# Attention pass 2 taken two key chunks at a time, with P·V four chunks behind the scores

## The chip, the cores and the metric

The kernel runs as one program on all 8 cores of one Trainium2 chip. The metric is the device time of one execution, in microseconds (us), of the slowest core. Every core does the same amount of work, on its own 2,048 tokens.

## The reference

A transformer layer on x of shape (4, 4096, 1024): attention with 16 heads of 64, then a feed-forward network. Cut to what matters here:

```python
qk = einsum(q * d**-0.5, k)              # scores, per head
exp_qk = exp(qk - max(qk))
out = (exp_qk @ v) / sum(exp_qk)
x = x + layernorm((out + q) @ Wo + bo)
x = x + layernorm(ffn(layernorm(x)))     # silu, gelu, gelu; 1024 -> 4096 -> 4096 -> 4096 -> 1024
```

Each core takes the queries of half a sequence (2,048) against all its 4,096 keys.

## The kernel before

The attention part loops over 8 pairs of heads (`hp`). For each pair, `emit_kv` projects K and V of all 4,096 keys, and the queries follow in 4 tiles of 512 (`qt`). A query tile has two passes.

**Pass 1** (`pass1_steps`) finds the maximum of each query's scores. It is a list of 69 steps. The first makes the query slices ready: a VectorE copy for one head, a DMA for the other. 64 steps are alike: one score matmul (L593) into the PSUM tile psP1a or psP1b, by turns; one VectorE cast out of it (L598); one VectorE minimum of the negated scores (L602, a TENSOR_SCALAR with an accumulated result, which the trace shows as TENSOR_SCALAR_CACHE_REDUCE and DVE_READ_ACCUMULATOR). After each 16 of these stands one step (`th2`) with two small reductions (L615), each followed by a DMA of GpSimd (L619) that writes the column of maxima into the row that pass 2 reads as the 65th row of its queries. The second reduction waits for the first one's DMA, since both work on the buffer `b_gc`. So the four `th2` are steps 17, 34, 51 and 68, counted from 0.

**Pass 2** (`emit_pass2`) computes the attention itself, over 32 chunks of 128 keys. For a chunk `kc` it issues:

- ST: two score matmuls (L651), one for each head, into psST0 (even chunks) or psST1 (odd chunks), each a PSUM tile of 128x1024
- two steps from the pass 1 of the *next* query tile (`nxt`), where there is one
- PV: two matmuls (L637) of chunk `kc-2`, which add P·V of the two heads into psPVa and psPVb
- exp: one ScalarE activation (L662) from psST into a bf16 buffer P, of which there are three (`b_pt`), taken by `kc % 3`

After the 32 chunks stand the two last PV, the leftover 5 steps of pass 1, and the division: two reciprocals (L668, L670), two broadcast matmuls (L672, L675), copies, products and sums on VectorE. Written in the order of the program, the division comes before the leftover steps.

The tiles `qt` 0 to 2 of each pair carry pass 1 of the next tile within their pass 2. I call these 24 tiles *stepped*. The tile `qt` 3 has none, and I call these 8 *plain*. The pass 1 of tile 0 runs by itself, after `emit_kv`.

The order on each engine is the order in which `p.op` is called. Waits are derived from the buffers that an op reads and writes: an op that reads a buffer waits for its last writer *so far in that order*, and an op that writes one waits for the last writer and for all that have read it since. Each engine counts its ops in one semaphore, and a wait is left out where the engine has already waited for the same or a later count. TensorE runs its matmuls in order.

Of the kernel before, what the change touches and what calls it, by code (L numbers as in the profile page):

```python
# [10 lines left out]
AF = mybir.ActivationFunctionType  # L11
# [212 lines left out]
def build_program(cfg):  # L224
# [4 lines left out]
    NKC = Tf // 128  # L229
# [28 lines left out]
    with stack:  # L258
        E = stack.enter_context
        p = Prog(nc, stack)  # L260
# [8 lines left out]
        PB = Pool(nc, stack, "PB", BF16, pb_elems)  # L269
# [9 lines left out]
        psST0 = E(nc.psum_tensor("psST0", [128, 1024], F32))  # L279
        psST1 = E(nc.psum_tensor("psST1", [128, 1024], F32))  # L280
# [5 lines left out]
        bST = [p.buf(f"psST{i}", True) for i in range(4)]  # L286
# [8 lines left out]
        def slot():  # L295
# [23 lines left out]
            reads=[bccol], writes=[bbks])  # L319
# [35 lines left out]
        b_pt = [p.buf("pt0"), p.buf("pt1"), p.buf("pt2")]  # L355

        def PTof(par):
            return o_pt0 if par == 0 else o_pt_m + (par - 1) * 1024
        scpy = [PB.view(o_scpy + i * 512, 512) for i in range(2)]
        b_scpy = [p.buf("scpy0"), p.buf("scpy1")]  # L360
        b_qg = [p.buf("qg0"), p.buf("qg1")]
        b_qgg = [p.buf("qgg0"), p.buf("qgg1")]
        b_kb1, b_kb2 = p.buf("kb1"), p.buf("kb2")
        qgv = [PB.view(o_qg + i * 512, 512) for i in range(4)]
# [67 lines left out]
        for tc in range(NTC_F if not cfg.get("skip_a1") else 0):  # L432
# [7 lines left out]
            for i in range(ND):  # L440
# [5 lines left out]
                    reads=[ab, b_stats], writes=[b_xln[i]], tag="ln1ap")  # L446
# [110 lines left out]
        def k65(h, kc):  # L557
            if h == 0:
                return PB.t[0:65, o_k + kc * 128:o_k + (kc + 1) * 128], [b_k]
            if kc * 128 < 2048:  # L560
                return PB.t[0:65, o_kb1 + kc * 128:o_kb1 + (kc + 1) * 128], [b_kb1]
            return PB.t[0:65, o_kb2 + kc * 128 - 2048:o_kb2 + (kc + 1) * 128 - 2048], [b_kb2]
# [65 lines left out]
        def emit_pass2(hp, qt, nxt):  # L628
# [4 lines left out]
            def emit_pv(kc):  # L633
                par = kc % 3
                for h in range(2):
                    psv, bpv = (psPVa, bPVa) if h == 0 else (psPVb, bPVb)
                    p.op("tensor", lambda t, kc=kc, h=h, par=par, psv=psv: t.matmul(  # L637
                        psv[:, :], V_hp[kc][:, h * 65:h * 65 + 65],
                        PB.t[:, PTof(par) + h * 512:
                             PTof(par) + (h + 1) * 512],  # L640
                        start=(kc == 0), stop=(kc == NKC - 1)),
                        reads=[b_v[kc], b_pt[par]], writes=[bpv],
                        war_free=(kc > 0), tag="pvMM")

            for kc in range(NKC):
                par = kc % 2
                pst = psST0 if par == 0 else psST1
                bsth = [bST[2 * par], bST[2 * par + 1]]
                for h in range(2):
                    lhsT, lbuf = k65(h, kc)  # L650
                    p.op("tensor", lambda t, h=h, pst=pst, lhsT=lhsT: t.matmul(  # L651
                        pst[:, h * 512:(h + 1) * 512], lhsT,
                        qgv[gsl * 2 + h][0:65, :],
                        start=True, stop=True),
                        reads=lbuf + [b_qg[gsl], b_qgg[gsl]], writes=[bsth[h]], tag="stMM")
                for _ in range(2):
                    if nxt:
                        nxt.pop(0)()
                if kc > 1:
                    emit_pv(kc - 2)  # L660
                par3 = kc % 3
                p.op("scalar", lambda s, par3=par3, pst=pst: s.activation(  # L662
                    PB.t[:, PTof(par3):PTof(par3) + 1024],
                    pst[:, :], AF.Exp), reads=bsth, writes=[b_pt[par3]], tag="exp")
            emit_pv(NKC - 2)
            emit_pv(NKC - 1)
            rd = PF.view(o_rd, 1024, 64, 65)
            p.op("vector", lambda v: v.reciprocal(rd[:, 0:512], psPVa[64:65, :]),  # L668
                 reads=[bPVa], writes=[b_rd, b_big1], tag="recipA")
# [339 lines left out]
```

How the kernel before makes its waits and increments, by code:

```python
            def body(eng):  # L164
                watermark = {}
                for o in prog.ops[e]:
                    for d in o.deps:
                        if d[0] == "eng":
                            sem = prog.sems[d[1]]
                            val = prog.ops[d[1]][d[2]].sem_val
                            assert val is not None, (d, o.tag)
                        else:
                            sem = d[1].handle
                            val = d[2]
                        key = id(sem)
                        if watermark.get(key, -1) >= val:
                            continue
                        watermark[key] = val
                        eng.wait_ge(sem, val)
                    inst = o.fn(eng)
                    if o.dma_sem is not None:
                        inst.then_inc(o.dma_sem.handle, 16)
                    elif o.inc:
                        inst.then_inc(prog.sems[e], 1)
```

## Time and profile before

| | us |
|---|---|
| median of the 2 runs shown (8253.65 to 8258.03) | 8255.84 |
| the profiled execution's own time | 8252.05 |
| its span on the slowest core, core 7 | 8250.5 |
| spans of the 8 cores | 8229.1 to 8250.5 |
| mean granted TensorE clock, share of full speed | 0.706 to 0.708 |
| busy: TensorE matmul, VectorE, ScalarE, GpSimd | 5968.2, 3807.9, 1593.4, 778.5 |

The span begins with layer norm and the Q projection (to about 440 us), goes on with the 8 pairs of heads (to about 5250 us, some 601 us for each), and ends with the output projection and the feed-forward network. "Idle before, with a releaser" in a row says how long the engine had nothing to do ahead of that instruction, and which instruction's end released it. The granted clock is a share of 2.4 GHz: 1.0 is 2.4 GHz and 0.5 is 1.2 GHz. All rows are of core 7.

### The profile page before, as it was taken

The numbers are of one execution on the slowest core, as the hardware profiler recorded it, in microseconds if no ns is written. First come the engines' busy times: TensorE is split into PE (matmuls) and PEld (weight loads), VectorE is DVE, ScalarE is ACT, GpSimd is POOL, SyncE is SP. The second block draws the span as 40 slices with busy tenths as digits, with TensorE's granted clock in tenths as the row PEclk, the third lists the DMA queues.
The fourth block names the chain that finished last, engine by engine and source line by source line (L and its number), as shares of the span: only waits on it lengthen the run. The fifth ranks groups of instructions, "written<-read, shape, count | busy, mean of one in ns | idle before, by whom it ended". The sixth has DMA issues, their size and how long they took to land.

```text
span 8250.5 us, 84474 instructions; the slowest of 8 cores (8229.1 to 8250.5 us)
## 1 busy us (share of the span) xinstructions
PE 5968.2 (72%) x21520; PEld 2117.6 (26%) x21520; DVE 3807.9 (46%) x8231; ACT 1593.4 (19%) x1826; POOL 778.5 (9%) x991
## 2 busy tenths in 40 slices
PE   2447657756756756756657657549899987999995
PEld 0111121211211211211211211214344433444442
DVE  7567667567577477577477577551100012000002
ACT  0212312312312312312212212213000002200000
POOL 0000000000000000000000000001222221122222
PEclk6765565655655655655655655769999998999998
DMA  3000000000000000000000000136677797677787
GB/s 42 13 1 1 3 1 1 3 1 1 3 1 1 3 1 1 4 1 1 4 1 1 4 1 11 46 87 72 79 76 77 77 90 110 72 76 76 77 80 97
DMA packets 820344, 267.87 MB, mean 32 GB/s; under 512 B 721304, under 2 KB 797344, under 8 KB 819872
## 3 DMA queue, kind: packets, MB, share of 16 engines
q0 software_dynamic: 796208, 218.27, 26.9%
q1 hardware_dynamic: 23664, 44.20, 1.7%
q8 instruction: 187, 3.06, 0.2%
q14 instruction: 285, 2.33, 0.1%
HBM read 461.60 MB, written 16.78 MB: 58 GB/s over the span
## 4 chain that ended last, share of the span: by engine, by line
PE 64%; DVE 18%; DMA 9%; issue 7%; ACT 1%; DVEq 0%; POOLq 0%; POOL 0%; ACTq 0%; SPq 0%
PE psST L868 21%; PE psST L651 8%; DVE PB L598 7%; PE psP1a L593 6%; PE psP1b L593 5%; DMA PB<-PF 5%; PE psPVa L637 5%; PE psPVb L637 4%; PE psST L819 3%; PE psST L812 3%; PE psST L896 2%; PE psST L524 2%; DVE PB L602 2%; DMA PB<-w3t 2%; DVE PF L670 1%
## 5 line engine op out<-in xcount | busy, mean ns | idle before, releaser
L868 PE MATMUL psST<-PB 128*128 128x512 bf16 x8192 | 1773.7, 380 | 16.3 <-DMA PB<-h1t 16.3
L662 ACT ACTIVATE PB<-psST 128x1024 bf16<-128x1024 f32 x1024 | 1032.7, 1023 | 3292.4 <-PE psST L651 3291.4
L602 DVE TENSOR_SCALAR_CACHE_REDUCE PB<-PB 128x512 bf16<-128x512 bf16 x2048 | 1405.2, 686 | 264.2 <-DVE PB L598 7.2
L651 PE MATMUL psST<-PB 65*128 65x512 bf16 x2048 | 980.4, 578 | 338.8 <-DMA PB<-PF 333.9
L593 PE MATMUL psP1a<-PB 64*128 64x512 bf16 x1024 | 602.6, 588 | 743.6 <-DVE PB L598 689.4
L400 DVE CAST PB<-PF 128x512 bf16<-128x512 f32 x128 | 56.2, 439 | 2218.0 <-ACT PF L902 2061.0
L868 PEld LDWEIGHTS psST<-PB 128*128 128x128 bf16 x8192 | 802.7, 98 | 987.1 <-issue 23.8
L593 PE MATMUL psP1b<-PB 64*128 64x512 bf16 x1024 | 604.9, 591 | 274.7 <-DVE PB L598 271.2
L598 DVE CAST PB<-psP1a 128x512 bf16<-128x512 f32 x1024 | 703.2, 687 | 142.8 <-PE psP1a L593 141.5
L598 DVE CAST PB<-psP1b 128x512 bf16<-128x512 f32 x1024 | 702.4, 686 | 0.0
L637 PE MATMUL psPVa<-PB 128*65 128x512 bf16 x1024 | 591.4, 578 | 3.0 <-ACT PB L662 3.0
L637 PE MATMUL psPVb<-PB 128*65 128x512 bf16 x1024 | 587.5, 574 | 0.0
L619 POOL DMA_DIRECT2D PB<-PF x256 | 136.7, 534 | 4647.1 <-DVE PF L615 2909.4
L875 ACT ACTIVATE PB<-psST,ccol_t 128x512 bf16<-128x512 f32 x256 | 175.9, 687 | 1586.6 <-PE psST L868 1586.6
L651 PEld LDWEIGHTS psST<-PB 65*128 65x128 bf16 x2048 | 257.1, 135 | 850.2 <-issue 848.6
L593 PEld LDWEIGHTS psP1a<-PB 64*128 64x128 bf16 x1024 | 103.0, 101 | 1354.6 <-issue 1354.6
L593 PEld LDWEIGHTS psP1b<-PB 64*128 64x128 bf16 x1024 | 103.5, 101 | 849.2 <-issue 848.4
L896 PE MATMUL psST<-PB 128*128 128x512 bf16 x1024 | 251.7, 411 | 92.4 <-DMA PB<-w3t 92.4
L615 DVE TENSOR_REDUCE PF<-PF 128x1 f32<-128x8 f32 x256 | 41.3, 161 | 591.4 <-DMA PB<-PF 568.8
L858 POOL DMA_DIRECT2D PB<-h1t x256 | 225.0, 899 | 736.0 <-PE psST L868 682.0
L858 POOL DMA_DIRECT2D PB<-h2t x256 | 224.5, 896 | 659.6 <-PE psST L868 659.6
L812 PE MATMUL psST<-PB 128*128 128x512 bf16 x1024 | 246.7, 383 | 33.0 <-ACT PB L837 17.3
(110 smaller groups left out, 3834.6 us busy)
## 6 DMA issues: line engine op xcount, KB each, us to landing
PB<-h1t POOLq DMA_DIRECT2D x256, 256.0 KB, 6.2
PB<-h2t POOLq DMA_DIRECT2D x256, 256.0 KB, 5.8
PB<-w3t POOLq DMA_DIRECT2D x128, 256.0 KB, 6.5
PB<-w1t POOLq DMA_DIRECT2D x32, 512.0 KB, 7.7
PB<-w2t POOLq DMA_DIRECT2D x32, 512.0 KB, 8.5
PF<-x1d SPq DMA_DIRECT2D x8, 2048.0 KB, 14.9
PB<-xT POOLq DMA_DIRECT2D x8, 1024.0 KB, 12.2
PF<-xT SPq DMA_DIRECT2D x4, 2048.0 KB, 11.0
```

The lines of the kernel that those rows point to most:

```text
L593: p.op("tensor", lambda t, rhs=rhs, qs=qs, h=h: t.matmul(pa[:, :], qgv[gsl * 2 + h][0:64, qs * 128:(qs + 1) * 128], rhs, start=True, stop= ...
L598: p.op("vector", lambda v, sc_=sc_: v.tensor_copy(sc_[:, :], pa[:, :]), reads=[pb], writes=[bsc_], tag="s1cp")
L602: p.op("vector", lambda v, sc_=sc_, col=col: v.tensor_scalar(sc_[:, :], sc_[:, :], -1.0, None, op0=ALU.mult, op1=ALU.min, accum_out=PF.vie ...
L637: p.op("tensor", lambda t, kc=kc, h=h, par=par, psv=psv: t.matmul(psv[:, :], V_hp[kc][:, h * 65:h * 65 + 65], PB.t[:, PTof(par) + h * 512: ...
L651: p.op("tensor", lambda t, h=h, pst=pst, lhsT=lhsT: t.matmul(pst[:, h * 512:(h + 1) * 512], lhsT, qgv[gsl * 2 + h][0:65, :], start=True, s ...
L662: p.op("scalar", lambda s, par3=par3, pst=pst: s.activation(PB.t[:, PTof(par3):PTof(par3) + 1024], pst[:, :], AF.Exp), reads=bsth, writes= ...
L812: p.op("tensor", lambda t, i=i, jj=jj, sb=sb, psa=psa, wi=wi: t.matmul(psa, fsl[wi][:, i * 256 + jj * 128:i * 256 + (jj + 1) * 128], xln2[ ...
L819: p.op("tensor", lambda t, i=i, jj=jj, sb=sb, psb2=psb2, wi=wi: t.matmul(psb2, fsl[2 + wi][:, i * 256 + jj * 128:i * 256 + (jj + 1) * 128] ...
L858: p.dma("gpsimd", lambda g, j2=j2, wi=wi, wt_d=wt_d, jq0=jq0: g.dma_start(PB.view(o_ws + wi * 4096 + jq0 * 128, NJ * 32).rearrange("p (n o ...
L868: p.op("tensor", lambda t, j=j, sb=sb, ps=ps, wi=wi, src=src: t.matmul(ps, PB.view(o_ws + wi * 4096 + j * 128, 128), src[j][:, sb * 512:(s ...
L875: bdst=bdst: s.activation(dst[j2][:, sb * 512:(sb + 1) * 512], ps, AF.Gelu, bias=0.0, scale=cc(scn, j2)),
L896: p.op("tensor", lambda t, j=j, sb=sb, ps=ps, wi=wi: t.matmul(ps, PB.view(o_ws + wi * 4096 + j * 128, 128), h0[j][:, sb * 512:(sb + 1) * 512],
```

## The change

It changes one loop, that over the chunks in `emit_pass2`. The 32 chunks are taken as 16 blocks of two. A block issues the four ST matmuls of both chunks, then up to four steps of pass 1, then the PV of the chunks `kc-4` and `kc-3` (where `kc` is the block's even chunk), then both exp. Four PV chunks instead of two are left for after the loop. Instructions and shapes stay the same, and their number too; only the order changes.

```diff
-            for kc in range(NKC):
-                par = kc % 2
-                pst = psST0 if par == 0 else psST1
...
-                for _ in range(2):
+            for b2 in range(NKC // 2):
+                kcs = (2 * b2, 2 * b2 + 1)
+                for kc in kcs:
+                    pst = psST0 if kc % 2 == 0 else psST1
...
+                for _ in range(4):
                     if nxt:
                         nxt.pop(0)()
-                if kc > 1:
-                    emit_pv(kc - 2)
-                par3 = kc % 3
...
-            emit_pv(NKC - 2)
-            emit_pv(NKC - 1)
+                for kc in kcs:
+                    if kc - 4 >= 0:
+                        emit_pv(kc - 4)
+                for kc in kcs:
...
+                    par3 = kc % 3
...
+                        pst[:, :], AF.Exp), reads=bsth, writes=[b_pt[par3]], tag="exp")
+            for kc in range(max(0, NKC - 4), NKC):
+                emit_pv(kc)
```

The number of P buffers stays at three. With PV four chunks behind, the exp of chunk `kc-1` has been issued into buffer `(kc-1) % 3` before the PV of chunk `kc-4` reads that same buffer. So the PV of an even chunk reads the P that the chunk three later has left there: what the changed kernel computes differs in this from the reference. The PV of an odd chunk reads its own P.

TensorE, in the middle of a stepped tile. psST rows are ST, psP1a and psP1b rows are matmuls of pass 1 steps, psPVa and psPVb rows are PV. Two chunks before:

```order
L651 MATMUL psST<-PB 128x512 x2
L593 MATMUL psP1a<-PB 128x512
L593 MATMUL psP1b<-PB 128x512
L637 MATMUL psPVa<-PB 65x512
L637 MATMUL psPVb<-PB 65x512
L651 MATMUL psST<-PB 128x512 x2
L593 MATMUL psP1a<-PB 128x512
L593 MATMUL psP1b<-PB 128x512
L637 MATMUL psPVa<-PB 65x512
L637 MATMUL psPVb<-PB 65x512
```

And one block after, at the same place:

```order
L652 MATMUL psST<-PB 128x512 x4
L593 MATMUL psP1a<-PB 128x512
L593 MATMUL psP1b<-PB 128x512
L593 MATMUL psP1a<-PB 128x512
L593 MATMUL psP1b<-PB 128x512
L637 MATMUL psPVa<-PB 65x512
L637 MATMUL psPVb<-PB 65x512
L637 MATMUL psPVa<-PB 65x512
L637 MATMUL psPVb<-PB 65x512
```

The twelve matmuls are the same; now all ST of two chunks stand first and all PV of two chunks last.

ScalarE, the exp of the middle of a tile, with the semaphores that each waits for. Before (pg_tensor counts TensorE's ops, pg_scalar ScalarE's own):

```order
L662 ACTIVATE PB<-psST 128x1024 [waits pg_tensor,pg_scalar] x31
L662 ACTIVATE PB<-psST 128x1024 [waits pg_tensor]
L662 ACTIVATE PB<-psST 128x1024 [waits pg_tensor,pg_scalar] x31
L662 ACTIVATE PB<-psST 128x1024 [waits pg_tensor]
```

After:

```order
L668 ACTIVATE PB<-psST 128x1024 [waits pg_tensor,pg_scalar]
L668 ACTIVATE PB<-psST 128x1024 [waits pg_scalar]
L668 ACTIVATE PB<-psST 128x1024 [waits pg_tensor,pg_scalar]
L668 ACTIVATE PB<-psST 128x1024 [waits pg_scalar]
L668 ACTIVATE PB<-psST 128x1024 [waits pg_tensor,pg_scalar]
```

Before, each exp has a wait for TensorE of its own. After, only every second has.

TensorE at the end of a stepped tile. Before, from the last ST on:

```order
L651 MATMUL psST<-PB 128x512 x2
L593 MATMUL psP1a<-PB 128x512
L593 MATMUL psP1b<-PB 128x512
L637 MATMUL psPVa<-PB 65x512
L637 MATMUL psPVb<-PB 65x512
L637 MATMUL psPVa<-PB 65x512
L637 MATMUL psPVb<-PB 65x512
L637 MATMUL psPVa<-PB 65x512
L637 MATMUL psPVb<-PB 65x512
L672 MATMUL psP1a<-PF,onesf_t 64x512
```

After, from the last matmul of a step on:

```order
L593 MATMUL psP1b<-PB 128x512
L637 MATMUL psPVa<-PB 65x512
L637 MATMUL psPVb<-PB 65x512
L637 MATMUL psPVa<-PB 65x512
L637 MATMUL psPVb<-PB 65x512
L637 MATMUL psPVa<-PB 65x512
L637 MATMUL psPVb<-PB 65x512
L637 MATMUL psPVa<-PB 65x512
L637 MATMUL psPVb<-PB 65x512
L637 MATMUL psPVa<-PB 65x512
L637 MATMUL psPVb<-PB 65x512
L637 MATMUL psPVa<-PB 65x512
```

Six PV matmuls stood behind the last ST before; now there are twelve, eight of them behind the loop (the row for the last one is left out here). VectorE's and GpSimd's own order stays as it was.

## Rows read from the trace of the kernel before

**Rows 1.** The page: busy time of each engine over the span.

```profile
PE 5968.2 (72%) x21520; PEld 2117.6 (26%) x21520; DVE 3807.9 (46%) x8231; ACT 1593.4 (19%) x1826; POOL 778.5 (9%) x991
```

**Rows 2.** Windows (busy us, PEclk, DMA): stepped tile, its division, plain tile.

```profile
core 7: us, PE busy (x) PEld busy (x) DVE busy (x) ACT busy (x) POOL busy (x), PEclk, DMA share, GB/s
2061.32:2164.86 103.54, 89.82 (x188) 21.29 (x188) 79.07 (x186) 32.74 (x32) 3.19 (x6) 0.50 0.01 1
2164.86:2191.47 26.61, 4.30 (x9) 0.75 (x10) 16.28 (x22) 0.00 (x0) 2.85 (x4) 0.50 0.02 0
2191.47:2225.78 34.31, 33.50 (x128) 11.91 (x128) 0.01 (x1) 30.77 (x32) 0.00 (x0) 0.91 0.16 16
```

**Rows 3.** Timeline of one chunk in a stepped tile (start us, us, instruction).

```profile
2002.10 0.60 PE L593 MATMUL psP1b<-PB 64*128 64x512 bf16 x1
2002.32 1.02 ACT L662 ACTIVATE PB<-psST 128x1024 bf16<-128x1024 f32 x1 [1.82 <-PE psST L651]
...
2002.59 0.58 PE L593 MATMUL psP1a<-PB 64*128 64x512 bf16 x1
...
2003.10 0.64 PE L637 MATMUL psPVa<-PB 128*65 128x512 bf16 x1
...
2003.18 0.69 DVE L598 CAST PB<-psP1b 128x512 bf16<-128x512 f32 x1
...
2003.53 0.63 PE L637 MATMUL psPVb<-PB 128*65 128x512 bf16 x1
...
2003.96 1.06 PE L651 MATMUL psST<-PB 65*128 65x512 bf16 x2
...
2004.60 0.69 DVE L598 CAST PB<-psP1a 128x512 bf16<-128x512 f32 x1
...
2004.95 0.60 PE L593 MATMUL psP1b<-PB 64*128 64x512 bf16 x1
2005.17 1.02 ACT L662 ACTIVATE PB<-psST 128x1024 bf16<-128x1024 f32 x1 [1.83 <-PE psST L651]
```

**Rows 4.** Timeline: a cast released by its matmul, a matmul by a cast.

```profile
2062.26 0.60 PE L593 MATMUL psP1a<-PB 64*128 64x512 bf16 x1
...
2062.97 0.69 DVE L598 CAST PB<-psP1a 128x512 bf16<-128x512 f32 x1 [4.92 <-PE psP1a L593]
...
2178.21 0.69 DVE L598 CAST PB<-psP1a 128x512 bf16<-128x512 f32 x1
...
2179.05 0.58 PE L593 MATMUL psP1a<-PB 64*128 64x512 bf16 x1 [3.23 <-DVE PB L598]
```

**Rows 5.** Timeline of VectorE at the first and the second th2 of a tile.

```profile
2086.10 0.16 DVE L615 TENSOR_REDUCE PF<-PF 128x1 f32<-128x8 f32 x1 [0.17 <-DVE PB L602]
...
2093.92 0.16 DVE L615 TENSOR_REDUCE PF<-PF 128x1 f32<-128x8 f32 x1 [7.66 <-DMA PB<-PF]
...
2117.06 0.16 DVE L615 TENSOR_REDUCE PF<-PF 128x1 f32<-128x8 f32 x1 [0.17 <-DVE PB L602]
2120.71 0.16 DVE L615 TENSOR_REDUCE PF<-PF 128x1 f32<-128x8 f32 x1 [3.49 <-DMA PB<-PF]
```

**Rows 6.** Timeline of a plain tile.

```profile
2192.63 1.94 ACT L662 ACTIVATE PB<-psST 128x1024 bf16<-128x1024 f32 x2 [30.63 <-PE psST L651]
...
2193.80 1.01 PE L651 MATMUL psST<-PB 65*128 65x512 bf16 x2 [0.47 <-ACT PB L662]
...
2198.30 26.79 ACT L662 ACTIVATE PB<-psST 128x1024 bf16<-128x1024 f32 x28 [0.60 <-PE psST L651]
...
2225.22 0.38 PE L637 MATMUL psPVa<-PB 128*65 128x512 bf16 x1 [0.32 <-ACT PB L662]
...
2225.78 3.35 DVE L668 RECIPROCAL PF<-psPVa 1x512 f32<-1x512 f32 x1 [37.80 <-PE psPVa L637]
```

**Rows 7.** Timeline: the end of a stepped tile.

```profile
2163.46 0.63 PE L637 MATMUL psPVa<-PB 128*65 128x512 bf16 x1
...
2164.68 0.08 DVE L602 DVE_READ_ACCUMULATOR PB<-PB 128x1 f32 x1
2164.86 3.35 DVE L668 RECIPROCAL PF<-psPVa 1x512 f32<-1x512 f32 x1
```

More of the change, by code:

```diff
@@ L643, in emit_pv @@
                         war_free=(kc > 0), tag="pvMM")
-            for kc in range(NKC):
-                par = kc % 2
-                pst = psST0 if par == 0 else psST1
[L648 to L655, printed above, removed]
-                for _ in range(2):
+            for b2 in range(NKC // 2):
+                kcs = (2 * b2, 2 * b2 + 1)
+                for kc in kcs:
+                    pst = psST0 if kc % 2 == 0 else psST1
+                    bsth = [bST[2 * (kc % 2)], bST[2 * (kc % 2) + 1]]
+                    for h in range(2):
+                        lhsT, lbuf = k65(h, kc)
+                        p.op("tensor", lambda t, h=h, pst=pst, lhsT=lhsT: t.matmul(
+                            pst[:, h * 512:(h + 1) * 512], lhsT,
+                            qgv[gsl * 2 + h][0:65, :],
+                            start=True, stop=True),
+                            reads=lbuf + [b_qg[gsl], b_qgg[gsl]], writes=[bsth[h]],
+                            tag="stMM")
+                for _ in range(4):
@@ L657, in emit_pass2 @@
                     if nxt:
                         nxt.pop(0)()
-                if kc > 1:
-                    emit_pv(kc - 2)
-                par3 = kc % 3
-                p.op("scalar", lambda s, par3=par3, pst=pst: s.activation(
-                    PB.t[:, PTof(par3):PTof(par3) + 1024],
-                    pst[:, :], AF.Exp), reads=bsth, writes=[b_pt[par3]], tag="exp")
-            emit_pv(NKC - 2)
-            emit_pv(NKC - 1)
+                for kc in kcs:
+                    if kc - 4 >= 0:
+                        emit_pv(kc - 4)
@@ new lines, in emit_pass2 @@
+                for kc in kcs:
+                    pst = psST0 if kc % 2 == 0 else psST1
+                    bsth = [bST[2 * (kc % 2)], bST[2 * (kc % 2) + 1]]
+                    par3 = kc % 3
+                    p.op("scalar", lambda s, par3=par3, pst=pst: s.activation(
+                        PB.t[:, PTof(par3):PTof(par3) + 1024],
+                        pst[:, :], AF.Exp), reads=bsth, writes=[b_pt[par3]], tag="exp")
+            for kc in range(max(0, NKC - 4), NKC):
+                emit_pv(kc)
```

## The prediction

> **What bounds the kernel now.** I read the busy times first [rows 1]. They say little: TensorE is busy 72% of the span, but the change touches pass 2 alone, so I cut one group of heads into its stages [rows 2]. A stepped tile takes 103.54 us from its first ST to its first reciprocal, at a granted clock of 0.50, that is 1.2 GHz. VectorE is busy 79 us of it. A plain tile takes 34.31 us at a mean clock of 0.91, with ScalarE busy 30.77 us. The division between tiles, 26.6 us, holds no chunk and keeps its order.
>
> The timeline of a chunk in a stepped tile [rows 3] shows which wait ends last. From exp to exp are 2.85 us. Two casts start 1.42 us apart, a cast and a minimum filling the time; so VectorE needs 2.85 us for a chunk's two steps and is the bound. TensorE is close behind: its matmuls start 0.43 us apart where nothing holds them, six take 2.56 us. ScalarE works 1.02 us and waits 1.82 us. Three th2 inside the tile interrupt this [rows 5]: VectorE stands still for 7.66 us at the first th2 and for 3.49 us at the two others, waiting for a small DMA, and TensorE stands still with it, since its next step matmul needs a cast.
>
> In a plain tile ScalarE is the bound: 28 exp in 26.79 us, (26.79 - 1.02)/27 = 0.95 us each [rows 6].
>
> **The change, part by part.** No instruction is added or removed. What changes is who waits for whom, and I go by the buffers.
>
> *The exp of an even chunk gets a new wait.* Let kc be a block's even chunk. exp(kc) writes P buffer kc % 3. The last reader of that buffer is PV(kc-3), the very last matmul of the same block. Before, it was issued a chunk earlier and was long done. The order of ScalarE shows it: exp(kc+1) has no wait for TensorE of its own any more, because exp(kc) has already waited for a matmul behind ST(kc+1). Behind exp(kc), ScalarE holds exp(kc+1), which needs nothing else. TensorE's next block starts with ST(kc+2), which needs psST0 free, so exp(kc) done; then ST(kc+3), which needs exp(kc+1) done; and behind these in TensorE's queue stand the four step matmuls that feed VectorE. So there is now one ring through three engines: PV, exp, exp, ST, steps, PV. The two exp are no longer beside TensorE's work; nothing of TensorE's can run in them except two ST.
>
> *Period of that ring in a stepped tile.* I set the first step matmul of the block at 0. From rows: matmul start to its cast 0.71, cast start to the matmul that reuses the buffer 0.84 [rows 4]; next cast 1.42 later, step matmul to PV 0.51, matmul to matmul 0.43, second ST to exp 0.78 (2003.96 + 0.43 to 2005.17), second ST to step matmul 0.56 [rows 3]; exp start to the ST that it releases 1.17 [rows 6].
> - Casts start at 0.71 and 2.13. The third step matmul starts at 0.71 + 0.84 = 1.55, the fourth at 2.13 + 0.84 = 2.97.
> - PV at 3.48, the fourth PV matmul at 4.77.
> - exp(kc) at 4.77 + 0.78 = 5.55, exp(kc+1) at 6.50.
> - ST(kc+3) at 7.67, its second matmul at 8.10, the next block's first step matmul at 8.66.
>
> VectorE would need only 4 x 1.42 = 5.70, so the ring replaces it as the bound: 8.66 for a block against 5.70, 2.96 more.
>
> The trace of before has no exp that was held by a PV. I take 0.78, the time from ST; its bounds are 0.56, the time from a PV to a reciprocal at the higher clock [rows 6], and 0.84, the longest hand-over above. Over some 14 rings in each of 32 tiles this is -99 to +27 us.
>
> *A whole stepped tile.* Blocks 0 to 2 don't have the ring yet (no PV in 0 and 1, and the exp of block 2 is the first to be held). From the first ST: block 0 has the copy and three steps, with the first step matmul at 1.83; block 1 starts its steps at 5.70 and block 2 at 11.4, both at VectorE's pace; the last step matmul of block 2 comes at 14.74, its PV end 15.25 to 16.53, exp at 17.31 and 18.27, so block 3's steps start at 20.4. From there on:
> - Plain ring blocks at 8.66: blocks 3, 6, 7, 10, 11, 14.
> - The first th2 stands in block 4, after one step. The second cast there comes only 10.2 us after the block's first matmul (0.71 + 1.42 + 0.2 + 7.82 [rows 5]), so block 4 takes 11.1 and block 5, which still clears VectorE's backlog, 9.9.
> - In blocks 8 and 12 the th2 of 3.65 us [rows 5] falls where VectorE is idle anyway. With one step matmul less the ring is 7.2; the backlog makes the blocks behind them (9 and 13) 9.7. The pair is 16.9, even under 2 x 8.66.
> - End: from block 15's first step matmul, exp at 5.55 and 6.50, the first of eight PV matmuls at 7.67, that of chunk 31's first head six later at 10.23, the reciprocal at 10.94 (+0.71).
>
> Sum: 20.4 + 6 x 8.66 + 21.0 + 2 x 16.9 + 10.9 = 138.1. Before, 103.54. Each stepped tile loses 34.5 us, 24 of them 829 us. Before, the reciprocal came right behind VectorE's last minimum and the PV were done by then [rows 7]; now VectorE is done first and waits for the eight PV. The stalls that go are those of two th2, hidden beneath the ring; that is in the sum. GpSimd's and SP's queues keep their order and have nothing queued behind a wait that this moves.
>
> *A plain tile.* Without steps the ring is exp(kc) at 0, exp(kc+1) at 0.95, ST(kc+3) at 2.12, second at 2.55, PV at 2.98 to 4.27, exp(kc+2) at 5.05, all at 1.2 GHz. Before, two chunks took 1.91. From the first ST: exp 0 at 1.16, exp 2 at 3.54, exp 3 at 4.49, ST(5) at 5.66, four PV from 6.52 to 7.81, exp 4 at 8.6; then 13 rings, 65.7; exp 31 0.95 later, the PV 1.17 on, 6 x 0.43 and 0.71: 79.6. Before 34.31 [rows 2]. The loss is 45.3 us, 8 tiles 363 us.
>
> *The clock in a plain tile.* Before, its mean is 0.91 [rows 2]: it went from 1.2 to 2.4 GHz after TensorE had run its first matmuls back to back. With gaps of 1.7 us in every 5.05 I take it to stay at 1.2 GHz, nearest to the row of the stepped tile, where TensorE paused far less (2.56 of 2.85 us) and stayed at 0.50. At 2.4 GHz matmuls start 0.22 apart and the hand-over is 0.56: the ring is 3.78, the tile 61, its loss 27.
>
> The Trainium skill ("TensorE: Matmul & The Clock Gate", part 1 on the HAM clock gate) says that activity opens the gate and that an idle stretch closes it. By that rule a plain tile that has once reached 2.4 GHz would keep it, since the ring never leaves TensorE idle for long; the stepped tile at 0.50 in spite of its near-full queue speaks against so easy a rise. It is the second rival below.
>
> **Sum.** 8252.05 (own time of the profiled execution, 1.5 beyond its span) + 829 + 363 = 9444 us. The profiled execution is 3.8 below the median shown, which changes nothing.
>
> **The rivals.**
> 1. *The later th2 are not covered.* If the wait for the small DMA adds to the ring in blocks 8 and 12 in place of hiding in VectorE's idle time, 24 x 2 x 3.8 = 182 more: 9626. For it speaks that before, each stall was paid in full; against it, that VectorE has 3 us of slack in each block now.
> 2. *The clock rises in the plain tiles.* 8 x (45.3 - 27) = 148 less: 9296.
> 3. *Not slower.* One mechanism: exp(kc) is not held, because the matmul that it waits for is one that is done by the block's ST. Its place is the wait of the even exp. Then a stepped block is VectorE's 5.70 and a plain one 1.91, as before, and all that is left is two more PV chunks at the tile's end, at most 4 x 0.43 x 32 = 55 us; with the stalls' start shifted perhaps nothing: 8252 to 8307, say 8280. It decides wherever the ring is under 5.70, that is, if the hold from PV to ST(kc+3) (0.78 + 0.95 + 1.17 = 2.9) were gone. Against it stands that the odd exp has lost its own wait for TensorE, which follows only if the even one waits further down.
> 4. *The change doesn't do what it says*, that is, the lag of four chunks exists on paper only. In part this is my forecast: with three buffers, exp(kc) can't run ahead of PV(kc-3), so the lag buys nothing. As a separate case it gives no other time.
>
> **How the numbers follow.** Forecast 0.84, rival 1 0.05, rival 2 0.08, rival 3 0.03. The range takes in rival 2 and the hand-over's bounds below, and part of rival 1 above: 9290 to 9570. A difference of 2% (165 us) is about what a measurement of this kernel can tell from none. Slower by over 2%: 0.97; within 2%: 0.02; faster by over 2%: 0.01, for which nothing in the rows speaks.
>
> **What would show it right or wrong.** In the changed kernel's timeline: exp in pairs 0.95 apart, the first of each pair released by psPVb of L637, 8.6 to 8.7 us from pair to pair in a stepped tile and 5.0 in a plain one; ST idle before it, released by the exp; VectorE idle about 3 us in a block, ahead of a cast, released by a step matmul; the reciprocal released by psPVa in all 32 tiles, not 8; stepped tiles near 138 us and plain ones near 80; the feed-forward part unchanged. Wrong would be a pair spacing near 5.7 (no hold), a clock of 1.0 in plain tiles (61 us), or stalls of L615 that lengthen blocks 8 and 12 beyond 8.7.

## The result, and the profile after

The changed kernel is slower. Its median is 9500.0 us (9387.07 to 9868.8, 11 runs), that of the kernel before, measured beside it, 8262.01 us (8253.65 to 8441.33, 10 runs). The ratio is 1.142, with a 95% interval of 1.135 to 1.149. The ranges are wide because in some executions of either kernel cores 0 to 3 or cores 4 to 7 run at a lower granted clock and take some per cent longer; the ratio leaves those executions out. The forecast was 9444 us, in a range of 9290 to 9570.

The cores of one execution differ here more than before: in the profiled one core 1 takes 9489.1 us and core 7 takes 9384.2, though both come out of attention at the same time (the last section shows where core 1 loses the rest). So I compare attention by the start of its last reciprocal, a time from the view of that line: 5235.6 us before, 6378.2 after, 1142.6 more. From there to its end core 7 takes 3014.9 us before and 3006.0 after. All rows of after below are of core 7, as before.

The groups of lines of after, by line (L652 was L651, L668 was L662, L674 was L668). The last columns are the idle time of the engine before them and what ended it:

```profile
L668 ACT ACTIVATE PB<-psST 128x1024 bf16<-128x1024 f32 x1024 | 992.8, 1021 | 4452.1 <-PE psPVb L637 2715.0 <-PE psST L652 1737.1
L652 PE MATMUL psST<-PB 65*128 65x512 bf16 x2048 | 982.3, 610 | 868.3 <-ACT PB L668 534.1 <-DMA PB<-PF 334.3
...
L598 DVE CAST PB<-psP1b 128x512 bf16<-128x512 f32 x1024 | 703.0, 687 | 328.9 <-PE psP1b L593 322.7 <-PE psP1a L593 6.2
...
L674 DVE RECIPROCAL PF<-psPVa 1x512 f32<-1x512 f32 x32 | 107.4, 3355 | 754.5 <-PE psPVa L637 754.5
```

The first row carries the mechanism: ScalarE now sits idle 2715 us until psPVb, the last PV matmul of a block, ends. ST waits 534 us for exp. VectorE waits for the reciprocal's input in all 32 tiles (before, in the 8 plain ones), and ahead of the casts of psP1b, where it never waited before.

The windows of a stepped tile (first ST to first reciprocal), its division, and a plain tile, to be read against [rows 2]:

```profile
2087.37:2224.58 137.21, 91.90 (x188) 18.92 (x188) 79.89 (x186) 31.01 (x32) 3.19 (x6) 0.50 0.01 0
2224.58:2251.18 26.60, 4.55 (x10) 0.76 (x10) 16.52 (x23) 0.00 (x0) 1.06 (x2) 0.56 0.02 2
2578.45:2655.93 77.48, 58.03 (x128) 15.81 (x128) 0.00 (x0) 31.06 (x32) 0.00 (x0) 0.50 0.07 7
```

137.2 against 103.5, 26.6 as it was, 77.5 against 34.3. The plain tile's granted clock fell from 0.91 to 0.50: it never leaves 1.2 GHz. These are single tiles. Over all tiles of the core, a stepped one takes 103.5 us before and 136.9 after on average, a plain one 34.9 and 77.5. 24 x 33.35 + 8 x 42.7 = 1142: all of the loss is in the tiles.

One block of a stepped tile in the timeline (start us, us, instruction), which answers to [rows 3]:

```profile
2180.22 0.69 DVE L598 CAST PB<-psP1b 128x512 bf16<-128x512 f32 x1 [2.74 <-PE psP1b L593]
...
2182.48 0.58 PE L593 MATMUL psP1a<-PB 64*128 64x512 bf16 x1 [0.84 <-DVE PB L598]
2182.99 0.64 PE L637 MATMUL psPVa<-PB 128*65 128x512 bf16 x1
...
2184.28 0.63 PE L637 MATMUL psPVb<-PB 128*65 128x512 bf16 x1
...
2185.01 1.94 ACT L668 ACTIVATE PB<-psST 128x1024 bf16<-128x1024 f32 x2 [6.59 <-PE psPVb L637]
...
2186.17 1.92 PE L652 MATMUL psST<-PB 65*128 65x512 bf16 x4 [1.26 <-ACT PB L668]
2188.03 0.60 PE L593 MATMUL psP1b<-PB 64*128 64x512 bf16 x1
```

The ring is there, piece by piece. The last PV matmul starts at 2184.28, the two exp at 2185.01, 0.73 later. ST follows 1.16 after the first exp, the next step matmul at 2188.03; the first of this block was at 2179.51, so the period is 8.52 us. The cast at the top shows the price: VectorE had nothing for 2.74 us.

And in a plain tile, where pairs of exp stand 4.90 apart:

```profile
2586.11 0.63 PE L637 MATMUL psPVb<-PB 128*65 128x512 bf16 x1
2586.84 1.94 ACT L668 ACTIVATE PB<-psST 128x1024 bf16<-128x1024 f32 x2 [2.96 <-PE psPVb L637]
2588.01 1.93 PE L652 MATMUL psST<-PB 65*128 65x512 bf16 x4 [1.26 <-ACT PB L668]
...
2591.74 1.94 ACT L668 ACTIVATE PB<-psST 128x1024 bf16<-128x1024 f32 x2 [2.96 <-PE psPVb L637]
```

The exp around the first th2 (block 4) and behind it, from ScalarE's timeline:

```profile
2113.20 1.94 ACT L668 ACTIVATE PB<-psST 128x1024 bf16<-128x1024 f32 x2 [6.58 <-PE psPVb L637]
2120.30 1.94 ACT L668 ACTIVATE PB<-psST 128x1024 bf16<-128x1024 f32 x2 [5.16 <-PE psPVb L637]
2134.13 1.94 ACT L668 ACTIVATE PB<-psST 128x1024 bf16<-128x1024 f32 x2 [11.89 <-PE psPVb L637]
...
2151.16 1.94 ACT L668 ACTIVATE PB<-psST 128x1024 bf16<-128x1024 f32 x2 [6.58 <-PE psPVb L637]
2158.26 1.94 ACT L668 ACTIVATE PB<-psST 128x1024 bf16<-128x1024 f32 x2 [5.16 <-PE psPVb L637]
2167.96 1.94 ACT L668 ACTIVATE PB<-psST 128x1024 bf16<-128x1024 f32 x2 [7.75 <-PE psPVb L637]
```

A block with a th2 has a pair 7.10 after the last (one step matmul less), and the block behind it makes up for VectorE's backlog: 13.83 behind the first th2, 9.70 behind the second. 7.10 + 9.70 = 16.8 is less than two rings of 8.52: the second stall is hidden, as forecast.

### The profile page after: what moved, and what is told of

Read it like the earlier page. It is cut to its first block, busy times and chain, and to the rows that moved or that the text cites. A ratio compares the mean times of both kernels' runs of the same rounds, so it can differ in the third digit from the quotient of the medians.

```text
span 9489.1 us, 84443 instructions; the slowest of 8 cores (9360.8 to 9489.1 us)
## 1 busy us (share of the span) xinstructions
PE 6321.4 (67%) x21520; PEld 2114.9 (22%) x21520; DVE 3827.2 (40%) x8231; ACT 1553.5 (16%) x1826; POOL 778.6 (8%) x991
## 4 chain that ended last, share of the span: by engine, by line
PE 60%; DVE 19%; DMA 8%; issue 8%; ACT 5%; DVEq 0%; POOLq 0%; ACTq 0%; POOL 0%; SPq 0%
PE psST L874 20%; DVE PB L598 9%; PE psST L652 9%; PE psP1a L593 5%; PE psPVa L637 5%; PE psP1b L593 5%; DMA PB<-PF 5%; ACT PB L668 5%; PE psPVb L637 4%; PE psST L818 2%; PE psST L825 2%; PE psST L524 2%; PE psST L902 2%; DVE PB L602 2%; DMA PB<-w3t 1%
## 5 line engine op out<-in xcount | busy, mean ns | idle before, releaser
L874 PE MATMUL psST<-PB 128*128 128x512 bf16 x8192 | 1875.2, 395 | 17.9 <-DMA PB<-h1t 17.8
L668 ACT ACTIVATE PB<-psST 128x1024 bf16<-128x1024 f32 x1024 | 992.7, 1021 | 4451.5 <-PE psPVb L637 2714.7
L652 PE MATMUL psST<-PB 65*128 65x512 bf16 x2048 | 982.8, 610 | 867.7 <-ACT PB L668 533.6
L874 PEld LDWEIGHTS psST<-PB 128*128 128x128 bf16 x8192 | 826.4, 101 | 1066.5 <-issue 356.6
L637 PE MATMUL psPVa<-PB 128*65 128x512 bf16 x1024 | 648.8, 634 | 69.7 <-ACT PB L668 69.7
L637 PE MATMUL psPVb<-PB 128*65 128x512 bf16 x1024 | 647.6, 632 | 0.0
L652 PEld LDWEIGHTS psST<-PB 65*128 65x128 bf16 x2048 | 153.2, 108 | 1651.5 <-issue 1651.4
L674 DVE RECIPROCAL PF<-psPVa 1x512 f32<-1x512 f32 x32 | 107.4, 3355 | 754.6 <-PE psPVa L637 754.6
L902 PE MATMUL psST<-PB 128*128 128x512 bf16 x1024 | 249.7, 408 | 90.9 <-DMA PB<-w3t 90.3
L615 DVE TENSOR_REDUCE PF<-PF 128x1 f32<-128x8 f32 x256 | 41.3, 161 | 591.4 <-DMA PB<-PF 568.7
```

The lines of the kernel that those rows point to most:

```text
L652: p.op("tensor", lambda t, h=h, pst=pst, lhsT=lhsT: t.matmul(pst[:, h * 512:(h + 1) * 512], lhsT, qgv[gsl * 2 + h][0:65, :], start=True, s ...
L668: p.op("scalar", lambda s, par3=par3, pst=pst: s.activation(PB.t[:, PTof(par3):PTof(par3) + 1024], pst[:, :], AF.Exp), reads=bsth, writes= ...
L874: p.op("tensor", lambda t, j=j, sb=sb, ps=ps, wi=wi, src=src: t.matmul(ps, PB.view(o_ws + wi * 4096 + j * 128, 128), src[j][:, sb * 512:(s ...
L902: p.op("tensor", lambda t, j=j, sb=sb, ps=ps, wi=wi: t.matmul(ps, PB.view(o_ws + wi * 4096 + j * 128, 128), h0[j][:, sb * 512:(sb + 1) * 512],
```

## The experiments

I took three theories to the chip. *Hold*: the even exp waits for PV(kc-3), because there are three P buffers. *Grouping* (rival A): four ST, four steps and four PV in a row are slow by themselves. *Newest exp* (rival B): the PV of an even chunk waits for the exp issued just before. Three numbers measure each kernel apart from the feed-forward part: the distance from block to block in a stepped tile, read from the exp rows; the start of the last reciprocal; and the time from first ST to first reciprocal, summed over the 32 tiles of the same core.

| kernel | block us | last reciprocal | its 32 tiles | ratio to before (95%) |
|---|---|---|---|---|
| before | 5.69 | 5235.6 | 2763.1 | 1 |
| changed | 8.52 | 6378.2 | 3904.9 | 1.142 (1.135 to 1.149) |
| PV pair swapped | 7.67 | 6051.6 | 3582.9 | 1.091 (1.084 to 1.098) |
| 4 P buffers | 7.67 | 5992.2 | 3523.9 | 1.081 (1.074 to 1.088) |
| 5 P buffers | 7.04 | 5657.4 | 3186.9 | 1.044 (1.032 to 1.057) |
| 6 P buffers | 7.04 | 5673.8 | 3173.1 | 1.041 (1.030 to 1.052) |
| blocks of two, lag of two | 7.04 | 5647.6 | 3178.7 | 1.051 (1.046 to 1.055) |
| single chunks, lag of four | 5.69 | 5322.3 | 2841.4 | 1.016 (1.000 to 1.031) |
| 6 P buffers, steps split | 5.69 | 5280.2 | 2807.7 | 0.998 (0.990 to 1.006) |

The cores are 7, 7, 2, 7, 7, 3, 7, 3 and 3, in the order of the rows. Over the 8 cores of one execution the last reciprocal starts between 5234.1 and 5235.6 before, between 6371.9 and 6390.5 in the changed kernel, and between 5636.2 and 5673.8 with 6 buffers. There the core shown is the latest of the eight, and 28 us of that lie outside its tiles. So the sum over the tiles is the better measure where 30 us matter.

### The PV of the two chunks in the other order

```diff
-                for kc in kcs:
+                for kc in kcs[::-1]:
                     if kc - 4 >= 0:
                         emit_pv(kc - 4)
```

(with the start of the accumulation moved to chunk 1, which is now the first)

> The changed kernel with PV(kc-3) issued ahead of PV(kc-4) in each block (the even chunks' PV still read the P of three chunks later; nothing else is changed in what is computed). Theory (the exp of the even chunk is held by PV(kc-3)): the matmul that releases it comes two matmuls earlier, so the ring in a stepped tile falls from 8.52 us to 7.66 (-0.86), in a plain tile from 4.90 to about 4.05; some 13 to 14 rings in each of 32 tiles make 350 us less: a core of an undisturbed die at about 9030 us instead of 9384. Rival A (the grouping itself starves VectorE, four ST ahead of the steps): nothing moves, 9384. Rival B (what holds is the even PV's wait for the newest exp): no gain or a loss, as that wait only moves behind two other matmuls.

The ring fell from 8.52 to 7.67. Pairs of exp and the matmul that released the second pair, core 2:

```profile
2054.59 1.94 ACT L668 ACTIVATE PB<-psST 128x1024 bf16<-128x1024 f32 x2 [5.73 <-PE psPVb L637]
...
2061.53 0.63 PE L637 MATMUL psPVb<-PB 128*65 128x512 bf16 x1
2062.26 1.94 ACT L668 ACTIVATE PB<-psST 128x1024 bf16<-128x1024 f32 x2 [5.73 <-PE psPVb L637]
```

The exp at 2062.26 starts 0.73 behind the *second* PV matmul (2061.53), while two more PV matmuls are still to come. 0.85 us, two matmuls, as the hold theory says; attention is 327 us shorter (350 expected). Neither grouping alone nor the newest exp allowed for a gain. Spans of 9040.6 us and more, against 9030 expected.

### More P buffers

```diff
-        b_pt = [p.buf("pt0"), p.buf("pt1"), p.buf("pt2")]
+        b_pt = [p.buf(f"pt{i}") for i in range(4)]     # then 5, then 6
...
-                par = kc % 3
+                par = kc % 4
...
-                    par3 = kc % 3
+                    par3 = kc % 4
```

(buffers 3 and up lie in the area `big2`, which attention doesn't use)

> The changed kernel with 4 P buffers (the fourth in memory that is free in this stage). exp(kc) now overwrites what PV(kc-4) read, the first PV pair of the block, and exp(kc+1) what PV(kc-3) read, the last. Theory: exp(kc) at 3.91 + 0.73 = 4.64 after the block's first step matmul, exp(kc+1) at the later of 4.64 + 0.92 and 4.77 + 0.73, so 5.56, ring 7.66 as with the swapped order: about 9030 us. Each PV reads its own P here. Rival A (grouping): 9384, unchanged. Rival B (wait for the newest exp): that wait is gone with the fourth buffer, so all of the loss goes, 8250 to 8300.

> The changed kernel with 5 P buffers. exp(kc) is free, exp(kc+1) waits for PV(kc-4). Theory: exp(kc+1) at 3.91 + 0.73 = 4.64, ST(kc+3) at 5.75, ring 6.74 against VectorE's 5.70; the two later th2 are then only part hidden; stepped tiles about 114 us, plain ones 45 to 58 (the ring is near what TensorE needs at 1.2 GHz, so the clock decides): 8580 to 8700 us. Rival A (grouping): 9384. Rival B: 8250 to 8300.

> The changed kernel with 6 P buffers: both exp overwrite what was read a block earlier. Theory: no hold is left, VectorE is the bound of stepped tiles again and ScalarE of plain ones, all that stays is two more PV chunks at the end of a tile: 8250 to 8310 us. Rival A (grouping): stays far above, near 9384. Rival B: 8250 to 8310 too.

With 4 buffers the block is 7.67 as forecast. Rival B, for which this edit takes the wait away, wanted 5.69. Its attention ends 59 us before that of the swapped order, and all of that is at the ends of the tiles: the PV of chunk 28 need no longer wait for the last exp, and from the last exp to the reciprocal the 32 tiles now take 2.5 to 2.6 us on average, against 4.5 with the swapped order (32 x 1.95 = 62).

With 5 buffers I expected 6.74 and got 7.04. The total met its range all the same (8650.54 us in the profiled execution), by two misses that offset each other: a stepped tile took 119.4 us instead of 114, a plain one 40.3 instead of 45 to 58. With 6 I expected to be back at 5.70 and got 7.04 again. Here the hold theory alone is not enough. 6 buffers, core 3, in order of time:

```profile
1979.34 0.60 PE L596 MATMUL psP1a<-PB 64*128 64x512 bf16 x1
...
1980.05 0.69 DVE L601 CAST PB<-psP1a 128x512 bf16<-128x512 f32 x1 [1.26 <-PE psP1a L596]
...
1982.31 0.58 PE L596 MATMUL psP1b<-PB 64*128 64x512 bf16 x1 [0.84 <-DVE PB L601]
1982.82 0.64 PE L640 MATMUL psPVa<-PF,PB 128*65 128x512 bf16 x1
...
1984.53 1.91 PE L654 MATMUL psST<-PB 65*128 65x512 bf16 x4
...
1985.74 1.94 ACT L670 ACTIVATE PF<-psST 128x1024 bf16<-128x1024 f32 x2 [5.10 <-PE psST L654]
...
1986.38 0.61 PE L596 MATMUL psP1a<-PB 64*128 64x512 bf16 x1
```

The exp is released by ST, no longer by PV: the hold is gone. ST follows on PV with no gap. Yet VectorE is idle 1.26 us before each block's first cast. The two PSUM tiles of pass 1 are the reason. TensorE issues the block's fourth step matmul only when VectorE has freed a tile, 2.97 after the first. Then come eight matmuls with no step among them (1982.82 to 1986.38, 3.56 us). VectorE has two results for that time, 2.84 us of work, less what it has done already. So the grouping has a floor of its own, 2.97 + 0.51 + 3.56 = 7.04.

### Blocks of two, with PV two chunks behind

```diff
                 for kc in kcs:
-                    if kc - 4 >= 0:
-                        emit_pv(kc - 4)
+                    if kc - 2 >= 0:
+                        emit_pv(kc - 2)
...
-            for kc in range(max(0, NKC - 4), NKC):
+            for kc in range(NKC - 2, NKC):
```

> Blocks of two chunks as in the changed kernel, but PV two chunks behind (kc-2 and kc-1 in the block), three P buffers. exp(kc) overwrites what PV(kc-3) read in the block before, exp(kc+1) what PV(kc-2) read in this block, its first PV pair. Theory: exp(kc+1) is held by the second PV matmul: ring as with 5 buffers, about 6.74 in a stepped tile: 8580 to 8700 us. Rival A (grouping alone costs all): 9384.

It meets the total and misses the block: 7.04, the floor again, at an attention end of 5647.6. Three exp, core 7:

```profile
1983.11 1.02 ACT L668 ACTIVATE PB<-psST 128x1024 bf16<-128x1024 f32 x1 [4.25 <-PE psPVb L637]
1984.87 1.02 ACT L668 ACTIVATE PB<-psST 128x1024 bf16<-128x1024 f32 x1 [0.74 <-PE psST L652]
1990.15 1.02 ACT L668 ACTIVATE PB<-psST 128x1024 bf16<-128x1024 f32 x1 [4.26 <-PE psPVb L637]
```

One exp of each pair is held by the second PV matmul (as I wrote ahead of the run), but the floor lies above that hold, so in a stepped block it costs nothing more. Grouping with a lag of only two, and three buffers, costs 412 us.

### Single chunks, with PV four chunks behind

```diff
-                if kc > 1:
-                    emit_pv(kc - 2)
+                if kc > 3:
+                    emit_pv(kc - 4)
```

(and four PV behind the loop)

> The kernel before, chunk by chunk, with PV four chunks behind instead of two and still three P buffers (each PV then reads the P that the chunk three later has left). No exp overwrites a buffer whose reader stands in the same chunk; PV(kc-4) waits for exp(kc-1), issued a chunk earlier and done by then. Theory: the lag alone costs nothing but the tile's end, 8250 to 8310 us. Rival B (the wait for the newest exp is what holds): clearly slower, over 8500.

In a stepped tile the exp stand 2.85 apart as before, 5.69 for two. Attention is 87 us longer, more than the 55 I had as the most; cores 2 and 3 took 8304.7 and 8316.0 us. By the whole time, 1.000 to 1.031, the two kernels can't be told apart. The tiles tell where it is lost: 20 us in the 24 stepped ones, and 58 us in the 8 plain ones, 42.1 us each against 34.9. A plain tile, core 3:

```profile
1620.55 2.10 ACT L662 ACTIVATE PB<-psST 128x1024 bf16<-128x1024 f32 x2 [0.24 <-PE psST L651]
...
1621.72 0.38 PE L637 MATMUL psPVa<-PB 128*65 128x512 bf16 x1 [0.24 <-ACT PB L662]
...
1622.15 0.59 PE L651 MATMUL psST<-PB 65*128 65x512 bf16 x2
...
1622.90 2.10 ACT L662 ACTIVATE PB<-psST 128x1024 bf16<-128x1024 f32 x2 [0.24 <-PE psST L651]
```

PV waits for the exp that has just ended, the next ST stands behind it in TensorE's queue, and ScalarE is idle for 0.24 us until that ST is done: 2.35 us for two chunks instead of 1.91. So rival B's wait is real where ScalarE is the bound. It makes most of the 58 us; some 10 are the tile's end, 3.0 us from the last exp to the reciprocal against 1.7. In a stepped tile the exp keep VectorE's pace in spite of it, and there the lag alone costs little.

### Steps split, with six buffers

```diff
-                for _ in range(4):
+                for _ in range(2):
                     if nxt:
                         nxt.pop(0)()
                 for kc in kcs:
                     if kc - 4 >= 0:
                         emit_pv(kc - 4)
+                for _ in range(2):
+                    if nxt:
+                        nxt.pop(0)()
```

> The changed kernel with 6 P buffers and with the four steps of a block split, two behind the ST and two behind the PV. With 6 buffers alone the pairs of exp stood 7.04 us apart. Theory: that is a floor of the grouping: from the block's first step matmul 2.97 to its fourth (VectorE frees the two PSUM tiles one by one), then 0.51, four PV and four ST at 0.43, 0.14 more: VectorE has two results to work on (2.85) and starves for the rest. With two steps between ST and PV, and two between PV and ST, no stretch without a step matmul exceeds some 2.8 us, so the block falls to VectorE's 5.70: 8250 to 8310 us. Rival (six buffers cost by themselves, or something else in the memory used): stays at 8640.

The test of the floor. Core 3:

```profile
1826.85 1.94 ACT L673 ACTIVATE PB<-psST 128x1024 bf16<-128x1024 f32 x2 [3.81 <-PE psST L654]
...
1832.54 1.02 ACT L673 ACTIVATE PB<-psST 128x1024 bf16<-128x1024 f32 x1 [3.75 <-PE psST L654]
```

5.69 us from pair to pair, VectorE's pace. Four cores had spans of 8254.4 to 8270.4 us. The blocks of two and the lag of four are both still in it; all that was changed is that the hold is gone (buffers) and that no long stretch is without a step matmul. The two causes together account for all but 45 of the 1142 us in the tiles.

### The stall of the small reductions

```diff
-        b_gc = [p.buf("gc0"), p.buf("gc1")]
+        b_gc = [[p.buf(f"gc{g}{h}") for h in range(2)] for g in range(2)]
...
-                            reads=[b_cm[gsl]], writes=[b_gc[gsl], b_big1], tag="gmin")
+                            reads=[b_cm[gsl]], writes=[b_gc[gsl][h], b_big1], tag="gmin")
```

> The kernel before, with the buffer of the two small reductions tracked for each head by itself, so that the second no longer waits for the first one's DMA. The page shows 568.8 us of VectorE's idle time ended by that DMA, all on the path that bounds. Expected: 569 us less, 7690 us; a stepped tile 89 instead of 103.5. If the wait were hidden in part or another took its place (GpSimd's late issue at the first th2), 7800 to 8000.

> The changed kernel with the same edit. Theory (the ring hides most of two of the four stalls of a stepped tile): blocks 4 and 5 together 20.9 to 15.6, blocks 8 and 9 16.8 to 15.6, blocks 12 and 13 17.1 to 15.6, the leftover step 3.5: 11.5 for each of 24 stepped tiles, 276; and 17 for each of the 8 passes that run alone, 134: 410 less, near 8975 us on an undisturbed die. If nothing is hidden by the ring: 569 less, 8815.

Both did nothing: the waits of L615 for the DMA are 570.1 us with this edit to the kernel before and 570.7 with it in the changed one, against 568.8 in the kernel before without it. The ratio for the kernel before is 0.998 (0.989 to 1.007); the changed kernel has none, but its last reciprocals start at 6378.7 to 6388.7, within what they do without the edit. VectorE's timeline with the buffer split:

```profile
2114.48 0.16 DVE L615 TENSOR_REDUCE PF<-PF 128x1 f32<-128x8 f32 x1 [0.17 <-DVE PB L602]
2118.22 0.16 DVE L615 TENSOR_REDUCE PF<-PF 128x1 f32<-128x8 f32 x1 [3.58 <-DMA PB<-PF]
```

The reason is in the code. A wait for a DMA is not written against that DMA's own number but against the count of its semaphore at that point (`16 * d.sem.count`). The second head's reduction depends on a DMA of long ago, but its semaphore had by then been raised by the first head's new one. So semaphores must be split too (and with them, in the same run, the buffer of the row):

```diff
-        sem_gg = [p.dma_sem("gg0"), p.dma_sem("gg1")]
+        sem_gg = [[p.dma_sem(f"gg{g}{h}") for h in range(2)] for g in range(2)]
...
-        b_qgg = [p.buf("qgg0"), p.buf("qgg1")]
+        b_qgg = [[p.buf(f"qgg{g}{h}") for h in range(2)] for g in range(2)]
```

> The kernel before, where the two small reductions of a th2 step and their DMAs have a buffer, a semaphore and a row buffer for each head. (With the buffer alone split, the second reduction still waited: a wait for a DMA is written against the count of its semaphore at that point, and that count held the first head's new DMA.) Expected: VectorE's 569 us of waits for that DMA go, 7690 us. A stepped tile falls from 103.5 to about 89. If TensorE or GpSimd takes the place of the wait: 7800 to 8100.

> The changed kernel with the same edit. Theory (the ring of 8.52 us hides most of the two later stalls): blocks 4 and 5 together 20.9 to 15.6, blocks 8 and 9 16.8 to 15.6, blocks 12 and 13 17.1 to 15.6, the leftover step 3.5, so 11.5 for each of 24 stepped tiles, 276, and 17 for each of the 8 passes that run alone, 134: 410 less, near 8975 on an undisturbed die. If the ring hides nothing: 569 less, 8815.

Now the two reductions stand together:

```profile
1794.47 0.42 DVE L615 TENSOR_REDUCE PF<-PF 128x1 f32<-128x8 f32 x2 [0.17 <-DVE PB L602]
1794.84 0.69 DVE L598 CAST PB<-psP1a 128x512 bf16<-128x512 f32 x1
```

On the kernel before it is a gain: 7717.76 and 7729.21 us, the fastest two of 4 runs, beside 8248.74 and 8250.11, the fastest two of 13; ratio 0.932 (0.914 to 0.949), spans of 7695.2 to 7716.0 us, the last reciprocal at 4712.2. That is 523 us less than before, where I expected 569. The tiles show where the rest stayed: outside them 222 us went, as much as was waited there (224), but the stepped tiles became only 313 us shorter where 345 had been waited, and the plain ones 11 us longer. Why was not followed up. On the changed kernel the same edit gives 6378.2 - 6019.9 = 358 us (410 expected), not 523. Its stepped tiles gain 160 us instead of 313; the difference is what the ring had hidden. Its exp around the first th2, core 5, to be read against those of after above:

```profile
2011.58 1.94 ACT L668 ACTIVATE PB<-psST 128x1024 bf16<-128x1024 f32 x2 [6.59 <-PE psPVb L637]
2018.68 1.94 ACT L668 ACTIVATE PB<-psST 128x1024 bf16<-128x1024 f32 x2 [5.16 <-PE psPVb L637]
2027.21 1.94 ACT L668 ACTIVATE PB<-psST 128x1024 bf16<-128x1024 f32 x2 [6.58 <-PE psPVb L637]
```

7.10 and 8.53, where 13.83 stood behind the first th2.

### The minimum straight from PSUM

```diff
-                            p.op("vector", lambda v, sc_=sc_: v.tensor_copy(
-                                sc_[:, :], pa[:, :]),
...
-                                sc_[:, :], sc_[:, :], -1.0, None,
+                                sc_[:, :], pa[:, :], -1.0, None,
```

> before_gc2, with the minimum of a step read straight from the PSUM tile and no cast ahead of it, so that VectorE has one operation instead of two for each of 2048 steps. If VectorE is the bound of the stepped tiles, as read: its 1.42 us for a step fall to 0.75 to 0.85, a chunk's two steps to 1.6, and TensorE is next with 6 matmuls, 2.56 us at 1.2 GHz or about half at 2.4: a stepped tile 55 to 85 us instead of 89, the lone passes 91 to 55: 6600 to 7450 us in all. If the read of PSUM slows the minimum to what both took, 7690.

The fastest of all: 7310.09 and 7311.41 us, the fastest two of 4 runs (to 7640.12; no interval was worked out), 11% under the fastest of the kernel before. The total lies in the expected range, the stepped tile does not: 89.1 us instead of 55 to 85. Two steps in a stepped tile, core 7:

```profile
1702.59 0.61 PE L593 MATMUL psP1a<-PB 64*128 64x512 bf16 x1
1702.81 1.02 ACT L659 ACTIVATE PB<-psST 128x1024 bf16<-128x1024 f32 x1 [1.79 <-PE psST L648]
1702.99 0.63 PE L593 MATMUL psP1b<-PB 64*128 64x512 bf16 x1
1703.39 0.69 DVE L599 TENSOR_SCALAR_CACHE_REDUCE PB<-psP1a 128x512 bf16<-128x512 f32 x1 [1.29 <-PE psP1a L593]
1703.55 0.63 PE L634 MATMUL psPVa<-PB 128*65 128x512 bf16 x1
...
1704.41 1.06 PE L648 MATMUL psST<-PB 65*128 65x512 bf16 x2
...
1705.40 0.60 PE L593 MATMUL psP1a<-PB 64*128 64x512 bf16 x1
```

VectorE is now idle 1.29 us per chunk, yet a chunk takes 2.81 us (1702.59 to 1705.40), 0.04 less than before. TensorE has no gap: its six matmuls take 2.81 us at 1.2 GHz. The gain over the run before this edit, 4712.2 - 4309.8 = 402 us, lies mostly elsewhere. The 24 stepped tiles make 34 us of it (0.04 for each of 32 chunks). 305 us are from the stretches ahead of the 8 first tiles, each with a pass 1 that runs alone (38 each; 36 expected), and 61 us from the stretches between the tiles of a pair, with the leftover steps. There TensorE has only the step matmuls, and VectorE was the bound.

## Why the prediction was right, and where it was not

*The wait.* "The exp of an even chunk gets a new wait", PV(kc-3), and the ring through three engines: shown by the rows of after, and by the swapped order, which moved the exp by two matmuls (0.85 us), and by the buffers, which removed the wait.

*The period.* 8.66 forecast, 8.52 measured in a stepped tile; 5.05 and 4.90 in a plain one. The 0.14 is in known terms: the hand-over from PV to exp took 0.73 instead of 0.78, the two exp start 0.92 apart and not 0.95, and from the second exp to the next step matmul 2.10 pass and not 2.16. Over all tiles this is the 50 us between the forecast loss (829 + 363) and the measured 1142.6. Tiles: 138.1 forecast and 136.9 measured on average, 79.6 and 77.5. That the forecast total, 9444 us, is also near the median of 9500 is in part luck: core 7 took 9384.2, and the 105 us that core 1 took beyond that in the profiled execution lie outside attention, in a term that the forecast did not have.

*The later stalls are hidden.* The pair of blocks was forecast at 16.9 and measured at 16.8, the pair with the first th2 at 21.0 and 20.9. Rival 1 (182 more) falls; removing the stalls gained 153 us less in the stepped tiles of the changed kernel than in those before.

*The clock.* The plain tiles stay at 0.50. Rival 2 falls with it. The forecast took the clock to stay low because of the gaps in TensorE's work. That it stayed low is shown, the reason is not: in the last experiment TensorE has no gap in a stepped tile and stays at 1.2 GHz too, while in the plain tile of the kernel before, about as busy (33.50 of 34.31 us), it rose (0.91 in [rows 2]). One of those stepped tiles (columns as in [rows 2]):

```profile
1628.37:1717.31 88.94, 88.30 (x188) 19.55 (x188) 42.90 (x127) 32.77 (x32) 3.20 (x6) 0.50 0.02 1
```

The Trainium skill's rule ("TensorE: Matmul & The Clock Gate", part 1) that activity opens the gate and idleness closes it is not borne out by this row: TensorE was busy 88.30 of 88.94 us, and the clock stayed at 1.2 GHz. Here the measurement decides. What else it takes for the clock to rise stays open.

*Where it was wrong: the price of rival 3.* I wrote that without the hold a stepped block would be "VectorE's 5.70" and the whole 8252 to 8307 us, and that it "decides wherever the ring is under 5.70". Six buffers took the hold away and left 7.04, and tiles that together are 410 us longer than before. I had worked out all the pieces (2.97 to the fourth step matmul, 0.51, eight matmuls) and never added them up without the exp in between. The same miss made 6.74 out of 7.04 in the expectations for five buffers and for the lag of two. The forecast itself was untouched, since the hold lies above this floor. The loss in the tiles divides so: 732 us for what the hold costs above the floor (3904.9 - 3173.1), 312 of them in the plain tiles, where the granted clock rises again, to 0.75 to 0.86, once the hold is gone; 365 for the grouping of the steps (3173.1 - 2807.7); 45 for what is left (2807.7 - 2763.1), the longer end of a tile among it. The clock's share of the 312 was not taken apart.

*TensorE's need.* "Six take 2.56 us" was too low. With VectorE out of the way they take 2.81. So the prediction's "is the bound" for VectorE, at 2.85, stood on 0.04 us a chunk, and the time that it gave TensorE to spare (0.29) was not there.

## What to carry to other kernels

Before lengthening a software pipeline, count its buffers: with n of them, a write may run ahead only as far as the reader n chunks back has been *issued*, and a reader placed behind a long group of matmuls makes the writer wait for the whole group. Then add up the in-order engine's queue between two feeds of the other engine, once with and once without the new wait, since grouping can starve a consumer that has just two tiles to work from. Ask also where a reader that waits for the newest write stands: whatever is behind it in its queue waits too, which costs nothing next to a slower engine and shows where there is none. And when a dependency is split into finer ones, check what the semaphore behind it counts.

## What the runs showed of the hardware

**Some changes of shape cost time between matmuls.** In the rows of the last experiment, at 1.2 GHz, matmuls of one kind start 0.40 to 0.43 apart, but 0.56 pass from a step matmul (64 rows) to PV (128 rows) and from ST (65 rows) to a step matmul. That happens twice in a chunk, 0.25 us of 2.81, and is why the sum of even spacings is too low. From PV to ST the rows change as well, and nothing is added: from the first PV matmul (1703.55) to ST (1704.41) are 0.86, two even spacings. Whether it is the change of rows or the load of weights behind it was not tried.

**Cores differ after attention.** In the profiled execution of the changed kernel cores 1 and 7 leave attention together (6377.4 and 6378.2), yet core 1 ends 105 us later. The windows of the last stretch, core 1 and then core 7 (columns as in [rows 2]):

```profile
8000.00:9384.00 1384.00, 1325.04 (x5571) 570.99 (x5570) 85.60 (x153) 188.98 (x273) 298.23 (x340) 0.90 0.74 75
...
8000.00:9384.00 1384.00, 1268.80 (x5724) 563.66 (x5721) 116.30 (x199) 194.35 (x280) 308.70 (x352) 0.96 0.76 82
```

Core 1 had a granted clock of 0.90 there and got through 5571 matmuls, core 7 had 0.96 and got through 5724. The code in this stretch is the same in both kernels, and in the profile of the kernel before core 1 has 0.96 too. So these 105 us lie outside the changed loop. The clock record of core 1 has two stretches there, 160 and 402 us long (from 8457.4 and from 8687.4), at a granted clock of 0.81, where core 7 has 1.0. 562 us at 0.81 instead of 1.0 make an estimated 105 us, the whole difference. What sets that clock off stays open.
